# A new order of the instructions in the main loop of a one-core AdaLN, Mamba-2 and mixture-of-experts kernel

## The reference, cut to what matters

```python
mod = (silu(c) @ wmod).reshape(8, 6, 1, 256); sa, ca, ga, sb, cb, gb = mod[:, 0..5]
h = layernorm(x) * (1 + ca) + sa
x = x + ga * mamba2(h)       # in-projection 256 -> 1288, depthwise conv of 4 taps, silu,
                             # state-space scan with 8 heads of 64 and state 128,
                             # times silu(z), RMS norm, out-projection 512 -> 256
h = layernorm(x) * (1 + cb) + sb
x = x + gb * moe(h)          # gates: softmax over 8 experts, those under 0.1 dropped,
                             # out = sum_e w_e * (h @ expert_w[e] + expert_b[e])
```

## Time and profile before

| what | value |
|---|---|
| median of 3 runs | 2277.26 us (2274.18 to 2278.06) |
| profiled execution, its own time | 2272.85 us |
| its span, first to last instruction | 2270.8 us |
| mean granted TensorE clock over the span | 0.973 |
| TensorE matmul busy | 2181.3 us, 96% |
| VectorE, ScalarE, GpSimd busy | 1893.8, 1788.6, 1620.3 us |

### The profile page before, as it was taken

One profiled execution on the slowest core, in us unless ns is written; L12 is line 12 of the kernel. 1 busy time (PEld: TensorE's weight loads), 2 busy tenths in 40 slices (PEclk: granted clock), 3 DMA queues, 4 the chain that ended last, 5 costly groups with the idle time before them and its releaser, 6 DMA issues. The chain is left out here.

```text
span 2270.8 us, 48650 instructions
## 1 busy us (share of the span) xinstructions
PE 2181.3 (96%) x14808; PEld 1874.0 (83%) x14808; DVE 1893.8 (83%) x4196; ACT 1788.6 (79%) x4208; POOL 1620.3 (71%) x1810
## 2 busy tenths in 40 slices
PE   4679999999999999999999999999999999999997
PEld 3568888888888888888888888888888888888875
DVE  4778898888898888898888889888889888889873
ACT  2678778888878788887788877788877788887872
POOL 1546777777777777777777777777777777777775
PEclk9789999999999999999999999999999999999999
DMA  4222122122122122122222212222212212212210
GB/s 119 70 71 67 60 78 80 59 79 83 58 69 83 60 82 79 58 66 83 70 73 78 71 60 78 70 70 78 79 57 73 83 58 83 80 57 67 73 54 19
DMA packets 154257, 160.86 MB, mean 71 GB/s; under 512 B 17200, under 2 KB 136592, under 8 KB 154000
## 3 DMA queue, kind: packets, MB, share of 16 engines
q1 hardware_dynamic: 148848, 157.71, 22.6%
q10 hardware_dynamic: 5152, 0.04, 0.1%
HBM read 139.88 MB, written 17.83 MB: 69 GB/s over the span
## 5 line engine op out<-in xcount | busy, mean ns | idle before, releaser
L897 DVE SCALAR_TENSOR_TENSOR feat<-pa,cw,feat 128x512 f32<-128x512 f32 x567 | 422.9, 746 | 39.2 <-ACT feat L603 24.8
L1300 PE MATMUL pe<-e_hi,h_hi 128*128 128x512 f32 x1024 | 450.7, 440 | 3.9 <-ACT ex L746 2.1
L1300 PE MATMUL pe<-e_hi,h_lo 128*128 128x512 f32 x1024 | 413.6, 404 | 0.0
L1300 PE MATMUL pe<-e_lo,h_hi 128*128 128x512 f32 x1024 | 412.5, 403 | 0.0
L1300 PE MATMUL pa<-h_hi,w_hi 128*128 128x260 f32 x1260 | 383.5, 304 | 10.3 <-DVE feat L897 9.1
L1300 PE MATMUL pa<-h_lo,w_hi 128*128 128x260 f32 x1260 | 357.5, 284 | 0.0
L1300 PE MATMUL pa<-h_hi,w_lo 128*128 128x260 f32 x1260 | 357.4, 284 | 0.0
L675 ACT ACTIVATE lm<-lm,lndt 128x128 f32<-128x128 f32 x1024 | 327.3, 396 | 1.7
L665 ACT ACTIVATE lm<-lm,e3in 128x128 f32<-128x128 f32 x1024 | 323.2, 403 | 4.1 <-DMA lm<-cs_rows 4.1
L1096 DVE SCALAR_TENSOR_TENSOR eacc<-pe,wg,eacc 128x256 f32<-128x256 f32 x512 | 245.0, 478 | 51.1 <-PE pe L1300 39.5
L439 POOL TENSOR_TENSOR rs<-ssq,neghalf 128x1 f32<-128x1 f32 x128 | 80.8, 632 | 280.3 <-DVE ssq L1004 280.3
(11 more groups left out here) (181 smaller groups left out, 6041.3 us busy)
## 6 DMA issues: line engine op xcount, KB each, us to landing
lm<-cs_rows SPq DMA_DIRECT2D x128, 512.0 KB, 3.9
ebc<-cs_rows SPq DMA_DIRECT2D x256, 128.0 KB, 3.0
xin<-_attn_hidden_states_dram SPq DMA_DIRECT2D x32, 512.0 KB, 4.1
xres<-_attn_hidden_states_dram SPq DMA_DIRECT2D x128, 128.0 KB, 3.3
out_dram<-x SPq DMA_DIRECT2D x128, 128.0 KB, 3.4
gz<-in_L_wmod_dram SPq DMA_DIRECT2D x2, 512.0 KB, 9.1
ex<-in_L_ffn_expert_w_dram SPq DMA_DIRECT2D x1, 1024.0 KB, 16.3
x<-in_L_ffn_expert_w_dram SPq DMA_DIRECT2D x1, 1024.0 KB, 17.8
```

Source lines behind the costliest of these rows:

```text
L897: dve.scalar_tensor_tensor(out=acc, in0=proj_bank(x, i)[:, :, 1 + j:1 + j + HT], scalar=cw[:, f, j:j + 1], in1=acc, op0=ALU.mult, op1=ALU. ...
L1300: return pe.matmul(o, lhsT=l, rhs=r, start=start, stop=stop, skip_group_check=True)
```

## The change

Only the order of the lists is changed, on all five engines; no step is added, dropped or altered, and no wait is. On TensorE the loop now runs to NTILE + 16 because `e2` of tile n - 9, which ended a pass, is now `e2` of tile n - 13 at the start of the next one; in return `ydiag_` of tile n - 7, second in a pass, is now `ydiag_` of tile n - 3, the last. So the head of a pass went from

The core of the diff, TensorE's list:

```diff
-            for n in range(0, NTILE + 12, T):
-                do(ss_, pe, n - 8)
-                do(ydiag_, pe, n - 7)
-                do(xT_, pe, n - 6)
-                do(gt_, pe, n - 12)
+            for n in range(0, NTILE + 16, T):
+                do(e2, pe, n - 13)
                 do(G_, pe, n - 6)
                 do(lgm_, pe, n - 10)
+                do(wout_, pe, n - 8)
                 do(dtm, pe, n - 4, T)
+                do(xT_, pe, n - 6)
+                do(ss_, pe, n - 8)
+                do(gt_, pe, n - 12)
                 do(e0, pe, n - 12)
-                do(wout_, pe, n - 8)
                 do(ft0, pe, n - 4, T)
+                do(wgT_, pe, n - 12)
                 do(yoff_, pe, n - 6)
-                do(wgT_, pe, n - 12)
+                do(bias_, pe, n - 12)
                 do(ydiag_, pe, n - 6)
-                do(bias_, pe, n - 12)
-                do(wout_, pe, n - 7)
+                do(e1, pe, n - 12)
                 do(state_, pe, n - 6)
                 do(ft1, pe, n - 4, T)
-                do(e1, pe, n - 12)
+                do(e2, pe, n - 12)
+                do(wout_, pe, n - 7)
...
                 do(state_, pe, n - 3)
-                do(e2, pe, n - 9)
+                do(ydiag_, pe, n - 3)
```

VectorE, head and tail of its list:

```diff
             for n in range(0, NTILE + 16, T):
-                do(M_, dve, n - 7)
                 do(ylo_, dve, n - 8)
                 do(h2hi_, dve, n - 10)
                 do(n_hi, dve, n - 2, T)
+                do(y3_, dve, n - 7)
                 do(S_, dve, n - 7)
-                do(y3_, dve, n - 7)
-                do(xD1, dve, n - 13)
+                do(red_, dve, n - 8)
                 do(n_st, dve, n, T)
                 do(n_st, dve, n + 1, T)
+                do(xD1, dve, n - 13)
...
                 do(xD0, dve, n - 9)
-                do(red_, dve, n - 4)
+                do(M_, dve, n - 3)
```

ScalarE, head of its list:

```diff
             for n in range(0, NTILE + 16, T):
-                do(yhi_, act, n - 8)
+                do(n_h, act, n - 2, T)
+                do(sq_, act, n - 8)
+                do(La, act, n - 6)
+                do(Lxa, act, n - 6)
+                do(Lb, act, n - 6)
+                do(gexp, act, n - 12)
                 do(xA1, act, n - 13)
-                do(n_h, act, n - 2, T)
-                do(La, act, n - 6)
-                do(Lb, act, n - 6)
-                do(Lxa, act, n - 6)
-                do(gexp, act, n - 12)
                 do(Lxb, act, n - 6)
+                do(gtE, act, n - 12)
+                do(sq_, act, n - 7)
+                do(yhi_, act, n - 7)
                 do(bt_, act, n - 6)
                 do(xt_, act, n - 6)
-                do(sq_, act, n - 7)
-                do(yhi_, act, n - 7)
-                do(gtE, act, n - 12)
```

More of the change, by code:

```diff
@@ L556, in _ @@
                 do(n_lo, pool, n + 2, T)
+                do(exb_, pool, n - 10)
                 do(scd_, pool, n - 2)
@@ L809, in _ @@
                 do(ca1, act, n - 4, T)
+                do(Lxa, act, n - 5)
+                do(xA0, act, n - 12)
                 do(Lb, act, n - 5)
-                do(xA0, act, n - 12)
+                do(ln_w, act, n - 4, T)
+                do(ca2, act, n - 4, T)
                 do(xt_, act, n - 5)
-                do(ln_w, act, n - 4, T)
-                do(Lxa, act, n - 5)
-                do(ca2, act, n - 4, T)
                 do(xA1, act, n - 12)
+                do(Lxb, act, n - 5)
                 do(sq_, act, n - 6)
+                do(xA0, act, n - 11)
                 do(csT_rows, act, n - 4, T)
-                do(Lxb, act, n - 5)
-                do(xA0, act, n - 11)
-                do(yhi_, act, n - 6)
[L822 to L826, removed]
+                do(si0, act, n - 4, T)
+                do(bt_, act, n - 5)
+                do(ca3, act, n - 4, T)
+                do(xA1, act, n - 11)
+                do(ln_dt, act, n - 4, T)
+                do(yhi_, act, n - 6)
                 do(ca4, act, n - 4, T)
@@ L829, in _ @@
                 do(bias_, act, n - 10)
+                do(Lb, act, n - 4)
                 do(sq_, act, n - 5)
@@ L843, in _ @@
                 do(xA1, act, n - 10)
+                do(La, act, n - 3)
                 do(xt_, act, n - 4)
@@ L850, in _ @@
                 do(xt_, act, n - 3)
+                do(xA0, act, n - 9)
                 do(Lxb, act, n - 3)
-                do(xA0, act, n - 9)
+                do(yhi_, act, n - 4)
                 do(bt_, act, n - 3)
-                do(sq_, act, n - 4)
                 do(h2, act, n - 6)
@@ L1228, in _ @@
                 do(tC1, dve, n - 4, T)
+                do(y4_, dve, n - 6)
+                do(sse_, dve, n - 7)
                 do(w1_, dve, n - 4, T)
-                do(y4_, dve, n - 6)
+                do(xD1, dve, n - 12)
+                do(x2_, dve, n - 7)
                 do(dts_, dve, n - 4, T)
-                do(sse_, dve, n - 7)
-                do(n_xn, dve, n, T)
-                do(xD1, dve, n - 12)
                 do(tA2, dve, n - 4, T)
@@ L1237, in _ @@
                 do(tC2, dve, n - 4, T)
-                do(st2_, dve, n - 8)
-                do(x2_, dve, n - 7)
+                do(n_xn, dve, n, T)
+                do(gs_, dve, n - 5)
                 do(y1_, dve, n - 5)
                 do(cse_, dve, n - 4, T)
+                do(st2_, dve, n - 8)
+                do(st2_, dve, n - 7)
+                do(M_, dve, n - 5)
                 do(ag2_, dve, n - 8)
-                do(red_, dve, n - 6)
-                do(st2_, dve, n - 7)
-                do(gs_, dve, n - 5)
+                do(ag2_, dve, n - 7)
                 do(xD0, dve, n - 11)
-                do(ag2_, dve, n - 7)
-                do(M_, dve, n - 5)
                 do(tA3, dve, n - 4, T)
@@ L1577, in _ @@
                 do(e3_, pe, n - 11)
-                do(ss_, pe, n - 6)
-                do(e2, pe, n - 11)
-                do(ydiag_, pe, n - 5)
-                do(ft4, pe, n - 4, T)
-                do(wout_, pe, n - 6)
-                do(bias_, pe, n - 10)
+                do(ydiag_, pe, n - 5)
+                do(e2, pe, n - 11)
+                do(ft4, pe, n - 4, T)
+                do(bias_, pe, n - 10)
+                do(e0, pe, n - 10)
+                do(wout_, pe, n - 6)
+                do(ss_, pe, n - 6)
                 do(G_, pe, n - 4)
-                do(e0, pe, n - 10)
+                do(state_, pe, n - 5)
                 do(h2T_, pe, n - 8)
```

134 lines of the change are left out of this document (65 added, 69 removed).

## The result

The changed kernel takes 2259.28 us (median of 8 runs, 2249.87 to 2267.38), the kernel before in the same comparison 2277.66 us (8 runs, 2274.18 to 2282.63). The ratio is 0.992 with a 95% interval of 0.9899 to 0.9942: 0.8% faster. The forecast was 1.6% faster, 2241 us. The direction and the mechanism of the gain were right and the time lies in the range, but only half of the forecast gain came. The profiled execution took 2257.78 us, its span is 2255.8 us.

A forecast was written before the change was run, and what follows sets the result against it. TensorE's stream, slowed by clock falls after runs of 16-column products, was taken as the bound. 36.8 us for falls plus 6.6 for `y3_`, less 3 for falls left and 4.5 for new waits, gave 36 less: 2241 us, range 2229 to 2262.

The forecast's parts named there:

- Start and end: Outside the 29 steady groups: waits kept, a fall or two may go there, up to 3 us less.
- New waits: Reordered queues, tightest at `xt_` for `yoff_(n - 6)`: 0.15 us a group, 4.5 us lost, bounds 0 and 15.
- What bounds the kernel: TensorE's own stream sets the time; its clock falls once in 23 of 29 groups, around `dtm`, after 2.7 us of 16-column products.
- The price of a fall: Steady groups: a fall costs 1.50 us, 1.53 with gates; all 23 gone gives 36.8 us.
- How many stay: Around `dtm`, whose 1.78 us is the new longest narrow run: two of 23 falls left, 3 us.
- rival A: Falls stay because transposes beside `dtm` do not hold the clock: in part 2250 to 2256 us, chance 0.2; whole 2271, 0.08.
- e0: TensorE step of wide products, in the new order behind `dtm`, `xT_` and `ss_`; the prediction counted it at 1.5 us.
- The rule on transposes: Skill's rule that transposes do not engage full clock, which would make falls stay; prediction set it aside, citing 17 transposes at 1.00.
- The wait for `y3_`: TensorE's `G_` waiting for `y3_`, 22 times 0.3 us: goes entirely, since `e2` now stands between; 6.6 us gained.
- one chain: From `lgm_` through `xt_` to `yoff_(n - 6)`: `xt_` ready at 9.2 to 9.4 us, TensorE there at 9.6, cover 0.2 to 0.4.
- The chances: Whole kernel: faster 0.89, same 0.05, slower 0.06; the forecast itself (2228 to 2249 us) 0.62.

The follow-up runs named there:

- x2: Changed kernel with `xt_(n - 3)` put before `n_h(n)` on ScalarE; 2253.45 us (median of 4), ratio 0.99.
- x6: Changed kernel with `wout_(n - 8)` moved in front of `lgm_`, so the 16-column products stand together again; 2295.42 us in a single run.
- x3: Kernel before with `wout_(n - 8)` moved between `lgm_` and `dtm`, and `y4_` and `dtb` swapped on VectorE; 2260.23 us, ratio 0.9925.
- a1: The changed kernel unaltered, executed and profiled a second time; 2269.74 us.
- a2: The changed kernel unaltered, executed and profiled a third time; 2255.07 us.
- x1: Changed kernel with the gates' product `gt_` moved behind `e0` on TensorE; 2255.94 us (median of 4), ratio 0.991.
- x5: Changed kernel with `xt_(n - 3)` before `n_h`, `gt_` behind `e0`, and `gtE` behind `xt_(n - 6)`; 2250.05 us (median of 4), ratio 0.99.
- x7: x2 with the gates' product over 128 rows instead of 8, the others zero, and 9 buffers instead of 10 for tile `x2`; 2250.88 us, single run.
- x8: x2 with `G_(n - 5)` moved from behind `xT_` to directly before `yoff_(n - 5)` on TensorE; profiled span 2259.3 us, single execution.

## Why the prediction was half right

The forecast of the steady part was 36 us; the three profiled executions of each kernel give 1959.7 and 1939.4 us in the mean, 20.2 less. Start and end were put at 0 to 3 us less; they are 7.6 us more. The medians of the runs differ by 18.4 us, half of the forecast 36.

The step that failed is the sum's account of what the new order costs. New waits stood in it with 4.5 us and cost about 12 (x2). TensorE's own stream was taken as equally long in any order, and cost about 11 more. Start and end were put at nothing to lose, and lost 7.6. The falls that stayed cost 7.6 and not 3. That the shortfall is no larger is luck: `y3_` was sized too small, 6.6 us for about 14, and that error went the other way.

- *What bounds the kernel.* Right. TensorE's clock parted the classes of groups, and the run of 16-column products made it fall: x6 brings 22 falls back with one moved step, x3 takes all but one away with one.
- *The price of a fall, 1.53 us.* Right: 68.97 against 67.40 us in the changed kernel, 67.84 against 66.34 in x6. Some falls are twice as long (70.46 in a1, 70.55 in x6) and cost 3.1.
- *How many stay.* Forecast 2 of 23, measured 2, 4 and 2. The number was right and the place was not: I feared `xT_` and `ss_` beside `dtm`, and no group with these alone fell: 22 groups in the profile and 21 each in a1 and a2, whose first group lies partly in the low clock of the start. It was `gt_`, which the prediction named in rival A only as a neighbour: behind `e0` it does no harm (x1, x5). That its 8 rows are what counts is likely (x7), and the form 8*128 stood in the trace. What is left costs 7.6 us in the mean of the three executions, with the first group's share of the start's low clock, and not 3.
- *The rule on transposes.* The Trainium skill ("TensorE: Matmul & The Clock Gate", Part 4: PE-mode transpose) would have had rival A as the outcome. The four transposes of `xT_` directly behind `dtm` did no harm, so here too the trace speaks against the rule; the measurement decides.
- *The wait for `y3_`.* Went as forecast, and was worth 0.56 us in a group without gates (`xT_` to `G_` 0.95 us, `xT_` alone 0.39) where I had read 0.30 off the gap.
- *New waits.* The term was mis-sized and misplaced. I counted one chain, to `yoff_(n - 6)`, and got it right: no wait shows there. The wait came at `yoff_(n - 3)`, at the other end of the pass, since `hT_` and `xT_`, which feed two neighbouring lines of ScalarE's list, traded places on TensorE: 0.41 us a group (x2), 11.9 us in all, against a forecast of 4.5. The gap that the profile shows for it, 6.5 us, is again only half of it.
- *The price of a new order with no wait in it.* This term was missing; I took TensorE's sum as independent of the order. It is not: `yoff_(n - 6)` and `yoff_(n - 5)` took 0.2 us more behind other neighbours, `G_(n - 4)` 0.17, `e1(n - 12)` 0.1, some others less. Together a quiet group without the wait for `xt_` is 65.94 us and not 65.57, 0.37 us or 10.7 us in 29 groups. The split between the two terms is rough, since x2 has a wait for `M_` of its own, about 0.1 us in a quiet group: by so much the neighbours cost less and the wait for `xt_` more. x8 shows one of these prices to be real, and also that the group does not follow when it is paid back.
- *Start and end.* Nothing was counted and 7.6 us were lost, and with them the small spread that the kernel before has. The view that would have warned was there: 95 us of start in which the engines wait for each other in an order written for it.
- *The gates.* Also missing: a group with gates is dearer by 1.05 us than one without (67.40 to 66.35), where it was 0.71 before (66.84 to 66.13), in seven groups 2.4 us. The trace shows why. Before, `gt_` stood between `xT_` and `G_` and lay over the wait for `y3_`: the earlier trace rows has 22 such waits, one for each group without gates, and none for the seven with them. Now there is no wait to cover, and the product costs its 1.05 us (302.36 to 303.41) in full.
- *The chances.* Those for a faster time add up to 0.90, not 0.89; nothing hangs on it.

In one sum, in the means of the three profiled executions of each kernel: 36.8 us for all falls of before, less 7.6 for what is left (the falls and what the low clock of the start adds to the first group), 16.2 (29 x 0.56) for `y3_`, less 11.9 for `xt_`, less 10.7 for neighbours, less 2.4 for the gates, which had covered part of the wait for `y3_` in seven groups, make 20.4 in the steady part, where 20.2 were measured. The terms for `xt_` and the neighbours are what the group lengths leave, so their sum is no proof of them. Less 7.6 for start and end, 12.8 us are left; the spans differ by 12.6 (2271.5 to 2258.9). The medians of the runs differ by more, 18.4, which is within the scatter of the changed kernel (a1 alone is 13 us above the mean of the other two).

## What to carry to other kernels

Put wide products between runs of narrow ones, and rather such as use all 128 rows (likely, x7). In this kernel one step in the right place did what the whole new order did, and one in the wrong place undid it. Then read each group without a clock fall by itself: a reordering pays in neighbours and in waits what it gains in clock, and the gap in front of an instruction understates a wait on TensorE, so compare the distance from step to step. And look at the start and the end for themselves: an order tuned for the full pipeline cost 7 us while this one filled.

## What the runs showed of the hardware

- Most falls in the steady groups have a price of 1.4 to 1.9 us, the longer ones 2.8 to 3.2; one short fall in x8 cost 2.7, and the one of x3, longer than all others, 4.2 over two groups.
- A product over 8 rows with 512 columns, its two records 0.53 us apart, is followed by a fall in 19 of 42 places; the same over 128 rows, 120 of them zero, in none of 7, of which two lie where the others fell (x7, one profiled execution).
- At the lower clock 16-column products do not stay at 0.11 us a start. The timeline of PE in the kernel before, where a fall begins in the middle of `dtm`:

```profile
159.56 0.26 PE L1300 MATMUL pa<-wdt,h_hi 128*128 128x16 f32 x1
159.67 0.26 PE L1300 MATMUL pa<-wdt,h_lo 128*128 128x16 f32 x1
...
160.18 0.36 PE L1300 MATMUL pa<-wdt,h_hi 128*128 128x16 f32 x1
160.39 0.36 PE L1300 MATMUL pa<-wdt,h_lo 128*128 128x16 f32 x1
```

They go from 0.11 to 0.21 us apart, so here the pace of narrow products halves with the clock too, though 256-column products start as close as 0.12 us at full clock, and a fall that lies over narrow products costs as much per us as one over wide ones.
